# Zeroing the unfilled rows of the image buffers: strips written by VectorE and GpSimd ahead of the first loads, in place of transfers of zeros

## The reference

```python
patches = X.reshape(B, C, 8, 28, 8, 28).transpose(0, 2, 4, 1, 3, 5).reshape(B, 64, 3*28*28)
tokens  = einsum('bpi,hi->bph', patches, W) + b            # 2352 -> 128
h = concat([cls, tokens], axis=1) * pos_embed              # 65 tokens an image
h = h + attn(layernorm(h), W_c)       # causal window of 64, softmax, sigmoid(concat @ W_c)
h = h + ffn(layernorm(h), ...)        # LayerNorm, router (16 experts, top 2), experts 128-512-128,
                                      # a shared expert, LayerNorm, 128-512-128
```

## Time and profile before

| | us |
|---|---|
| runs (3) | 1070.29, 1073.42, 1074.11; median 1073.42 |
| the profiled execution | 1070.02 |
| its span | 1068.3 |
| busy in the span | PE 914.3 (86%), PEld 748.4, DVE 655.2 (61%), ACT 580.6, POOL 435.3 |

### The profile page before, as it was taken

How to read it: one execution, slowest core, us unless ns; L and a number is a source line. 1 busy time by engine, 2 the same in 40 slices (tenths; PEclk the granted TensorE clock), 3 DMA queues, 4 the chain that set the end, 5 groups by cost and what they waited for, 6 DMA issues and landing times.

```text
span 1068.3 us, 21771 instructions
## 1 busy us (share of the span) xinstructions
PE 914.3 (86%) x5352; PEld 748.4 (70%) x5352; DVE 655.2 (61%) x2122; ACT 580.6 (54%) x1024; POOL 435.3 (41%) x399
## 2 busy tenths in 40 slices
PE   3168999999999999996508999999999858999996
PEld 2157777777777777775307999999999735556554
DVE  2205777777777777775337666666666346566553
ACT  2125566666666666663204556555655435666564
POOL 0001244545454545554461121222122278777770
PEclk9588999999999999998558999999999979999999
DMA  9778777777777777731168788888888322233231
GB/s 244 84 154 232 222 215 214 216 216 217 217 217 216 216 217 217 218 102 44 52 192 255 216 247 250 246 244 249 247 246 233 119 69 67 86 100 84 83 84 34
DMA packets 210743, 189.14 MB, mean 177 GB/s; under 512 B 16957, under 2 KB 185114, under 8 KB 210458
## 3 DMA queue, kind: packets, MB, share of 16 engines
q1 hardware_dynamic: 195136, 159.57, 54.0%
q0 software_dynamic: 12256, 27.81, 7.8%
q10 hardware_dynamic: 3322, 1.44, 0.5%
HBM read 150.15 MB, written 35.85 MB: 174 GB/s over the span
## 4 chain that ended last, share of the span: by engine, by line
PE 49%; issue 13%; POOL 13%; DVE 10%; SPq 10%; DMA 3%; ACT 2%; DVEq 0%; POOLq 0%; ACTq 0%
PE bank L1296 14%; PE bank L1433 13%; PE bank L1422 11%; POOL region L828 9%; SPq L383 7%; POOL rstd L761 3%; PE bank L1301 3%; PE bank L1411 2%; SPq L405 2%; DVE region L936 1%; PE bank L1331 1%; PE bank L1309 1%; DMA region<-y_rows,gidx 1%; DVE i L1024 1%; DMA region<-in_x 1%
## 5 line engine op out<-in xcount | busy, mean ns | idle before, releaser
L1296 PE MATMUL bank<-xf,wp 128*128 128x256 f32 x1280 | 315.8, 393 | 24.0 <-ACT xf L567 24.0
L1296 PEld LDWEIGHTS bank<-xf,wp 128*128 128x128 f32 x1280 | 236.0, 191 | 67.1 <-ACT xf L567 25.0
L761 POOL TENSOR_TENSOR rstd<-var,neghalf 128x4 f32<-128x4 f32 (+2 forms) x51 | 90.7, 1778 | 301.7 <-DVE var L927 199.5
L675 ACT ACTIVATE region<-bank,cols 128x256 f32<-128x256 f32 x320 | 135.1, 477 | 119.8 <-PE bank L1422 119.8
L567 ACT ACTIVATE xf<-region 128x1024 f32<-128x1024 f32 x160 | 173.9, 1133 | 46.8 <-DVE region L936 43.7
L777 POOL DMA_INDIRECT z_rows<-z,posg x130 | 150.4, 1157 | 37.6 <-issue 37.6
L1433 PE MATMUL bank<-region 128*128 128x128 f32 x1280 | 156.5, 276 | 0.0
L806 POOL DMA_DIRECT2D y_rows<-region x80 | 58.3, 728 | 234.4 <-DVE region L1114 225.2
L1433 PEld LDWEIGHTS bank<-region 128*128 128x128 f32 x1280 | 150.8, 193 | 0.0
L828 POOL DMA_INDIRECT region<-y_rows,gidx x130 | 129.3, 995 | 41.2 <-issue 36.9
L936 DVE COPY region<-region 32x1792 f32<-32x1792 f32 (+1 forms) x96 | 104.6, 1089 | 65.5 <-DMA region<-in_x 35.7
(11 more groups left out here) (173 smaller groups left out, 1154.1 us busy)
## 6 DMA issues: line engine op xcount, KB each, us to landing
region<-in_x SPq DMA_DIRECT2D x384, 196.0 KB
region<-in_L_ffn_ew SPq DMA_DIRECT2D x160, 256.0 KB, 3.5
region<-z_rows SPq DMA_DIRECT2D x80, 128.0 KB, 2.9
y_rows<-region POOLq DMA_DIRECT2D x80, 128.0 KB, 3.1
out<-region SPq DMA_DIRECT2D x65, 64.0 KB
ht_dram<-hT SPq DMA_DIRECT2D x16, 256.0 KB
r_dram<-rr SPq DMA_DIRECT2D x16, 256.0 KB
region<-ht_dram SPq DMA_DIRECT2D x16, 256.0 KB, 5.5
```

The lines of the kernel that those rows point to most:

```text
L675: act.activation(ehT[n % 2][:, c], bank[1 + c][:, 0:EROWS], ACT.Silu, bias=bias[c])\
L761: pool.tensor_tensor(dst, var, neghalf[:, 0:var.shape[1]], ALU.pow).then_inc(ready, 1)
L1296: ins = pe.matmul(out_cols, wp[:, s], cols_in, start=s == 0, stop=s == MAIN - 1)
```

## The change

The four transfers of zeros and the semaphores `gap_zeroed` are gone. In their place stand 16 memsets, one for each buffer and image: `zero_gap` writes partitions 64 to 95 of the image's 1792 columns. Of these, 64 to 83 are filled by the image's loads afterwards, and 84 to 95 keep their zeros. The third block copy now moves 32 partitions (64 to 95) and so carries zeros into 116 to 127. Because a strip covers partitions that the load fills, each image's first load must wait for its strip: SP waits, image by image, for the count of VectorE's strips or of GpSimd's. VectorE has 7 strips, GpSimd 9; `(g, b)` is buffer and image. The strips of `xb[1]` that lie over the weights come after `w_laid` or `wp_t`. `move_block(0, 0, 0, 0, j)`, the three copies of group 0's first half, is moved ahead of the class-token chain. The three warm-up matmuls are removed.

```diff
+DVE_GAPS = [(0, 0), (0, 2), (0, 4), (1, 4), (1, 6), (1, 0), (1, 2)]
+POOL_GAPS = [(0, 1), (0, 3), (0, 5), (0, 6), (0, 7), (1, 3), (1, 5), (1, 7), (1, 1)]
...
             lo, hi = BLOCKS[n]
             buf = half(k, u)
-            return buf[FOURTH:FOURTH + hi - lo, :, n * EXTRA:(n + 1) * EXTRA], buf[lo:hi, :, MAIN:PATCH]
+            hi = lo + P - FOURTH
+            return buf[FOURTH:P, :, n * EXTRA:(n + 1) * EXTRA], buf[lo:hi, :, MAIN:PATCH]
+
+        def zero_gap(eng, g, b, done):
+            w = XCOLS // GIMG
+            eng.memset(xb[g][2 * 32:FOURTH, b * w:(b + 1) * w], 0.0).then_inc(done, 1)
...
             def load_x(g, k, u):
                 for b in range(u * HIMG, (u + 1) * HIMG):
+                    if isinstance(g, int) and g < 2:
+                        for eng_zeroed, order in ((gap_zeroed_dve, DVE_GAPS), (gap_zeroed_pool, POOL_GAPS)):
+                            if (g, b) in order:
+                                sp.wait_ge(eng_zeroed, order.index((g, b)) + 1)
...
             load_x(0, 0, 0)
             load_x(0, 0, 1)
-            sp.wait_ge(memset_done, 2)
-            zero_gaps(0)
-            sp.wait_ge(wp_t, W_TILES)
-            zero_gaps(1)
             load_x(1, 1, 0)
             load_x(1, 1, 1)
+            sp.wait_ge(memset_done, 1)
...
         def _(pool):
-            pool.memset(neghalf[:, :], -0.5).then_inc(memset_done, 1)
+            pool.memset(neghalf[:, :], -0.5).then_inc(neghalf_set, 1)
+            pool.wait_ge(neghalf_set, 1)
+            for n in range(8):
+                zero_gap(pool, *POOL_GAPS[n], gap_zeroed_pool)
+            pool.wait_ge(wp_t, W_TILES)
+            zero_gap(pool, *POOL_GAPS[8], gap_zeroed_pool)
+            pool.wait_ge(gap_zeroed_pool, len(POOL_GAPS))
...
         def _(dve):
+            for n in range(3):
+                zero_gap(dve, *DVE_GAPS[n], gap_zeroed_dve)
+            dve.memset(wlaid, 0.0).then_inc(pads_zeroed, 1)
             dve.memset(ones[:, :], 1.0)
...
             dve.memset(rstd2[:, :], 1.0).then_inc(memset_done, 1)
-            dve.memset(wlaid, 0.0).then_inc(pads_zeroed, 1)
...
+            zero_gap(dve, *DVE_GAPS[3], gap_zeroed_dve)
+            zero_gap(dve, *DVE_GAPS[4], gap_zeroed_dve)
+            dve.wait_ge(w_laid, CH + CH * len(BLOCKS))
+            zero_gap(dve, *DVE_GAPS[5], gap_zeroed_dve)
+            for j in range(len(BLOCKS)):
+                move_block(0, 0, 0, 0, j)
+            dve.wait_ge(wp_t, W_TILES)
+            zero_gap(dve, *DVE_GAPS[6], gap_zeroed_dve)
             dve.wait_ge(ld_id, 16)
...
-                    if isinstance(g, int) and g < 2 and u == 0:
-                        dve.wait_ge(gap_zeroed[g], 32)
...
-            for g, u in ((0, 0), (0, 1), (1, 0)):
+            for g, u in ((0, 1), (1, 0)):
...
-            for _ in range(WARM):
-                pe.matmul(bank[1][:, :], a_bd[:, 0], a_bd[:, :].rearrange("p t d -> p (t d)"), start=True, stop=True)
             patch(0, 0, HALVES * UNITS)
```

More of the change, by code:

```diff
@@ L273, in build @@
         ld_id, ld_const, ld_w = sem("ld_id"), sem("ld_const"), sem("ld_w")
-        memset_done, dve_setup = sem("memset_done"), sem("dve_setup")
+        memset_done, neghalf_set, dve_setup = sem("memset_done"), sem("neghalf_set"), sem("dve_setup")
         cls_var, cls_rstd, xcls_ready = sem("cls_var"), sem("cls_rstd"), sem("xcls_ready")
@@ L280, in build @@
         xact_ready, block_moved, xunit_used = sem("xact_ready"), sem("block_moved"), sem("xunit_used")
-        gap_zeroed = [sem(f"gap_zeroed{u}") for u in range(2)]
+        gap_zeroed_dve, gap_zeroed_pool = sem("gap_zeroed_dve"), sem("gap_zeroed_pool")
         wp_ready = sem("wp_ready")
@@ L678, in _ @@
             act.wait_ge(tab_ready, 1)
-            act.wait_ge(memset_done, 2)
+            act.wait_ge(memset_done, 1)
+            act.wait_ge(neghalf_set, 1)
             act.activation(spare[:, :], neghalf[:, 0:1], ACT.Silu)
@@ L761, in rstd @@
                 pool.tensor_tensor(dst, var, neghalf[:, 0:var.shape[1]], ALU.pow).then_inc(ready, 1)
-            pool.wait_ge(memset_done, 2)
+            pool.wait_ge(memset_done, 1)
             for u in range(2):
@@ L857, in _, with move_block @@
         def _(dve):
+            def move_block(g, k, h, u, n):
+                if n == 0:
+                    dve.wait_ge(x_loaded[k][u], h * (16 * HIMG * CH) + 16 * HIMG * CH)
+                dst, src = block_parts(k, u, n)
+                dve.tensor_copy(dst, src).then_inc(block_moved, 1)
+            for n in range(3):
+                zero_gap(dve, *DVE_GAPS[n], gap_zeroed_dve)
+            dve.memset(wlaid, 0.0).then_inc(pads_zeroed, 1)
             dve.memset(ones[:, :], 1.0)
@@ L927, in attend_norm @@
                 dve.tensor_scalar(var1[:, :], mv[:, :, 1], EPS, None, ALU.add).then_inc(var1_ready, 1)
-            def move_block(g, k, h, u, n):
-                if n == 0:
-                    if isinstance(g, int) and g < 2 and u == 0:
-                        dve.wait_ge(gap_zeroed[g], 32)
-                    dve.wait_ge(x_loaded[k][u], h * (16 * HIMG * CH) + 16 * HIMG * CH)
-                dst, src = block_parts(k, u, n)
-                dve.tensor_copy(dst, src).then_inc(block_moved, 1)
             def body(r, k, h_, nt=GT, attn=True, ahead=2):
@@ L1279, in _ @@
             pe.wait_ge(ld_id, 16)
-            pe.wait_ge(memset_done, 2)
+            pe.wait_ge(memset_done, 1)
             pe.wait_ge(w_laid, CH + CH * len(BLOCKS))
@@ L1285, in _ @@
                     ins.then_inc(wp_t, 1)
-            WARM = 3
             def patch(g, lo, hi):
```

## The result

| | before | changed |
|---|---|---|
| median of the runs on the same chips, us | 1072.06 (4 runs) | 1037.66 (1036.5 to 1038.82, 4 runs) |
| ratio, 95% interval | | 0.9677 [0.9657, 0.9698] |
| profiled execution, its span, us | 1070.02, 1068.3 | 1037.49, 1035.8 |

The forecast was 1037, from a sum of -34.3 us. The medians differ by 34.4, the profiled executions by 32.5.

A forecast was written before the change was run, and what follows sets the result against it. SP's image loads and zero transfers were taken to bound the start, TensorE the rest of stage 1. -29.7 - 3.3 - 1.3 = -34.3 us on 1070.02 gives 1035.7, stated as 1037 for run spread; range 1031 to 1052.

The forecast's parts named there:

- start of `body(0)`: Group 0's attention in stage 1 would start at 52.2 instead of 81.89 us: -29.7.
- length of `body(0)`: Without cooled TensorE and the wait for group 1's second half, it takes 25.8 instead of 29.06 us: -3.3.
- length of `body(1)`: The wait for group 2's first loads goes, with SP ahead by then: 28.52 falls towards 27.18 us, -1.3.
- What bounds the kernel: Stage 1 bound by TensorE once running; its start by SP issuing image loads (63.1%) and zeros (15.4% of the chain).
- SP's queue: Four zero transfers, 17.06 us, go; first load at 2.55, then every 0.915; halves land by 19.3, 30.3, 41.3, 52.3.
- The strips: Memsets of 1792 elements a partition: 1.53 us on VectorE, 1.6 on GpSimd, 3.9 kept for the range.
- DVE and the weights: VectorE's set-up: three strips first, weight copies end at about 10.6; no cost, as ACT's copies release TensorE's transposes.
- Rival 1: GpSimd strips block VectorE's ten weight copies until the eighth strip ends: about 1 us, time 1038 to 1042; chance 0.14.
- The class-token chain: Moved image copies delay its start on VectorE from 17.42 to 24.1 us; ACT's image copies follow at 28.1.
- Group 0 and the loop: Last patch matmul at 51.4, `body(0)` at 52.2; removed warm-up takes 4.4 us off TensorE's line; later loads stay ahead.
- rival 2: GpSimd strips take 3.9 us, so `rstd` follows 12.5 later: 1050, or 1055 with the lock; chance 0.19 including values between.
- rival 3: Slower than before: port lock with GpSimd strips of 6.0 us or more eats the 34.3; 1077 at 6.5; chance 0.03.

The follow-up runs named there:

- experiment 8: Changed kernel, class-token chain first, GpSimd's sixth to eighth strips held until weight copies end, ninth until class-token row is normalised: 1032.78 us, ratio 0.9632.
- experiment 5: Changed kernel with GpSimd's sixth to eighth strips waiting until all weight copies are done: 1034.92 us, ratio 0.967 to the kernel before.
- experiment 4: Changed kernel with class-token chain before VectorE's three image copies, its rstd before GpSimd's ninth strip and stores: 1034.09 us, ratio 0.9661 to the kernel before.
- experiment 6: Changed kernel with all 16 strips on GpSimd, none on VectorE: 1041.88 us, ratio 0.973 to the kernel before.
- experiment 2: Kernel before without its three warm-up matmuls, nothing else: 1071.85 against 1071.27 us, ratio 1.0004.
- experiment 1: Changed kernel with the three warm-up matmuls put back ahead of group 0's patch matmuls: 1038.78 us, ratio 0.9704 to the kernel before.
- experiment 7: Changed kernel with each of GpSimd's nine strips written twice, on a slower chip: 1178.1 against 1204.5 us for the kernel before, ratio 0.9762.
- experiment 3: Kernel before with its four zero transfers issued from ScalarE's queue instead of SP's: 1062.54 us, ratio 0.9917.

## Why the prediction was right

The time was met, 1037 against 1037.66, and the mechanism was the one described. That it was met within 1 us is partly luck: the profiled execution gained 1.8 us less than the sum, and the 1.3 us put on top for the spread of the runs made up for most of it. Its terms, as measured between the earlier trace rows and the rows of after:

| term | predicted | measured |
|---|---|---|
| start of `body(0)` | -29.7 | 53.16 - 81.89 = -28.7 |
| length of `body(0)` | -3.3 | (78.79 - 53.16) - 29.06 = -3.4 |
| length of `body(1)` | -1.3 | (106.08 - 78.79) - 28.52 = -1.2 |
| all | -34.3 | -33.4; at the end of the execution -32.5 |

The second profile of the changed kernel (beside experiment 8) starts `body(0)` at 54.45 and gives -27.4 for the first row and -32.1 for the three together, so tenths in this table are not to be leaned on.

**What bounds the kernel.** Right: SP's queue and the slow zeros held TensorE, and after the loop everything only shifts. VectorE's last group starts at 461.97 instead of 495.63 (-33.7), the first gather of stage 3 at 815.91 instead of 851.25 (-35.3). The 2.8 us lost after that lie in stage 3: from its first gather to the end it took 217.1 us before and 219.9 after, but between 215.9 and 219.2 in the other profiles on ordinary chips (experiments 1 to 6 and 8), with no relation to the edit. So I read this as the spread of single executions; I did not test it.

**SP's queue.** First load at 2.86, not 2.55, since VectorE's first memset starts at 1.28; 48 loads in 43.78 us (0.912 each), ended at 46.64 against 46.5. No wait at a strip after the first. Group 0's two halves and the first of group 1 were copied by VectorE at 20.19, 30.75 and 40.99 against landings forecast at 19.3, 30.3 and 41.3.

**The strips.** GpSimd's took 1.58 us (1.6 taken; the 3.9 of the other row was far off). That is luck in part: the slope hung on the 6 ns between 98 and 104 for 7 elements, and one ns more or less would have moved the strip by 0.26 us. VectorE's took 1.55 (1.53), but with 0.32 us between two of them, which I had not counted: three strips and the gap to `wlaid`'s memset cost 5.93 us, not 4.6.

**DVE and the weights: the step that failed.** "The ten weight copies end at about 10.6 ... this costs nothing." They ended at 14.34 and TensorE's transposes waited for them until 14.48, 0.7 later than before. ScalarE's two copies, which released them before, here ended at 12.18 and would have let them start over 2 us earlier. Rival 1 was true as a mechanism: I had taken from the earlier trace rows that the VectorE copy keeps its time and GpSimd gives way; experiment 5 shows the other direction, 1.64 and 2.34 us where it is 0.46 and 0.99. By the Trainium skill (SBUF — State Buffer, "Who interferes with whom"), of a VectorE instruction in a two-port mode and a GpSimd one whoever issues first blocks the other fully. The trace agrees that either can be held (the earlier trace rows and these rows); which of two that start within 0.03 us wins, the recorded starts don't tell (experiment 4). Experiment 6 shows that it doesn't follow that every copy in a row waits. The delay was cheap because only two copies met a strip before the eighth was over, and the delay fell into VectorE's wait for images, as the rival's price of about 1 us said. It used that wait up: VectorE's third strip after the weights ended at 20.06, the images had landed at 20.16; in experiment 5, without the delay, VectorE waited 3.13 us there.

**The class-token chain.** It started at 25.79 instead of 24.1 (landing 0.9 later, the copies 3.59 instead of 3.3, gaps around the strip), and took 4.42 us to the end of ACT's copy instead of 3.96, since TensorE had idled and ran its small matmuls there at a granted clock of 0.50, where before it was 1.00 (L1401 took 0.79 us, L1386 before 0.49). That is the -29.7 turned into -28.7, after group 0's patches gave back 1.0 (22.28 us against 23.26). Experiment 4 shows that the place of the copies, named as the cost in the forecast, is worth 4.3 us (5.6 against the changed kernel's second profile).

**Group 0 and the loop.** Right: no wait for images inside `body(0)` or `body(1)`, then 27.17 us for `body(2)`. Removing the warm-up was worth 0 in the kernel before (experiment 2) and at most 1.3 us here (experiment 1), not the 4.4 that it takes on TensorE's line, because the matmuls behind it ran faster (9.23 us for the first half instead of 11.19 and 12.11).

**Rivals 2 and 3** did not occur. Experiment 7 makes a strip cost 3.2 us where nothing runs beside it (4.17 - 1.00) and 3.5 on average, and gets +7.3 us; the serial queue of rival 2 gives 1.0 + 9 x 3.5 + 1.68 = 34.2 for `rstd`, which came at 34.88. The slope of rivals 1 and 3, by which the weight copies are held until the eighth strip ends, is not sound: in experiment 7 they ended at 15.86, long before it, and in experiment 6 at 13.99. No strips were as slow as rival 3 needs, so its price stays untested; these two runs suggest that it was too high. In the prediction's estimate with strips of 3.0 us the sum should read -29.9 (1.0 + 9 x 3.0 + 1.68 is 4.4 over 25.3), not -29.7.

## What to carry over

Look first at a queue that one engine serves in order: there a slow transfer costs its own time and everything behind it, but experiment 3 shows that another queue recovers only part (8.7 of 34 us) when the transfer also takes the DMA engines' time. Work that an idle engine can do in 1.6 us pieces ahead of each transfer's deadline is nearly free, provided the queue in front of the next chained instruction (here `rstd` on GpSimd) still ends before it is wanted. When such a bound goes, put the short chain that everything waits for ahead of work that waits for data.

## What the runs showed of the hardware

- A float32 memset of 32 partitions x 1792 took 1.58 us on GpSimd and 1.55 on VectorE (changed kernel); successive ones stood 1.57 to 1.58 apart on GpSimd and 1.87 apart on VectorE.
- A VectorE copy and a GpSimd memset hold each other up: 3.33 us for three 32x1792 copies alone (experiment 5), 6.48 beside strips (experiment 6), while single strips stretch to 2.4 and 2.5 us (experiment 7).
- With all DMA engines busy (shares 0.98 and 0.99 from 30 to 40 us) the same image loads ran at 238 GB/s in one profile (experiment 4) and at 221 in another (experiment 8). Group 1's first half was copied at 40.14 and 43.35; in the two profiles of the unaltered changed kernel it was 40.99 (235 GB/s) and 43.46 (217).

- One chip ran both kernels far slower (1178.1 and 1204.5 us). Only experiment 7's was profiled there: from 200 to 300 us it moved 169 GB/s at a DMA share of 0.58 and a granted clock of 0.88, against 216, 0.75 and 1.00 in the changed kernel's profile. What limited it was not looked into.
